# A graph network on one Trainium2 core: PE's stop at every seventh select removed, POOL's gathers tied to the selects that DVE has taken

## The chip, the cores and the metric

The kernel runs on one core of one Trainium2 chip. The metric is the device time of one execution in microseconds (us), as the median of several runs. The engines are called PE (TensorE), DVE (VectorE), ACT (ScalarE), POOL (GpSimd) and SP (SyncE, which only issues DMAs here).

## The reference

There are 6250 nodes with 128 features each and 200,000 edges, sorted by their destination. Edge messages are combined in two blocks, each with a layer norm before it and a residual after it:

```python
h = relu(layernorm(x))                       # block 1, src/dst as row/col
e = relu(h[row] @ W1[:128] + h[col] @ W1[128:] + b1)
mask = sigmoid(e @ W2 + b2)                  # one number per edge
w = mask / (segment_sum(mask, row)[row] + 1e-9)
agg = segment_sum(w * h[col], row)
x = x + relu(where(deg > 0, 0.5 * h + 0.5 * agg, h) @ Wl + bl)

h = relu(layernorm(x))                       # block 2, four layers
for layer in range(4):
    agg = segment_max(h[src], dst)           # 0 where a node has no edge
    h = relu(agg @ W + b + h @ R)
x = x + h
```

## The kernel before

Nodes stand in 49 tiles of 128, grouped into 7 ranges of 7 tiles (896 nodes). The work comes in stages: lists of neighbours are built first; then the edge stage computes `mask` for each edge (the block of the program with names `a_...`, lines 1055 to 1545); then a stage sums the weighted neighbours (`b_...`); then the four layers of the max block run (`c_...`, lines 1853 to 2370).

The edge stage and each of the four layers fetch neighbour rows in two ways at once.

**Selects.** One neighbour of a node in each of the 49 source tiles is fetched by a matrix product with a 0/1 matrix, the choice. For every range (7) and every source tile (49) there is one select, so 343 in the edge stage and 343 in a layer. A select (`select`, L1316 and L2151) is six matmuls on PE, three parts of the features by two column blocks of 512 and 384, into a PSUM buffer `wide`: there are two such buffers in the edge stage and three in the layers. DVE then takes the result (`take`, L1404 and L2242), one 128x896 instruction on `hidden` or on `even`/`odd`, and counts the semaphore `taken` up by one. PE waits for `taken` before it writes the same buffer again. The choice matrices of seven selects form a chunk. Three chunk buffers exist. In the layers SP loads them from DRAM (`load_choice`); in the edge stage DVE makes them (`compare`). After the last select of a chunk PE waits for its own matmuls and then counts `choice_used` up, which is what frees the chunk buffer:

```python
last.then_inc(selected, 1)
if s % CHUNK == CHUNK - 1:
    pe.wait_ge(selected, n + 1)
    pe.sem_inc(choice_used, 1)
```

**Gathers.** The neighbours that selects don't cover are fetched by POOL with indirect DMAs (`gather_tile`, L1199 and L2032). Each gathers 128 rows of 512 bytes into one slot of a ring, and there are 430 of them in the edge stage and in a layer, 2 to 25 for a tile (`CAP`). POOL takes the tiles in order. Before a tile it waits only until the tiles that lay in its ring slots have been reduced. The ring has 38 slots in the edge stage and 56 in the layers, so POOL may run ahead of DVE by that much.

**Order of the work.** Each engine's order is written out by the Python loops. DVE goes through the selects; where the count of gathers reached in proportion to the selects, plus a lag of 5 selects, ends tile u, it waits for the tile's gathers to land and reduces it (`reduced_at`, `weigh_tile`, `reduce`). In the edge stage POOL also scatters the tile's mask values to DRAM, one indirect DMA for each of the 430 columns (`store_tile`, L1211), five tiles behind the gathers. In the layers POOL stores the new features of a range with seven indirect DMAs (`store`, L2049) after the gathers of the fourth tile of the next range; those features are made at the earliest 16 selects after the range's reductions end (`STAGED_AT`, `STEP`; for the sixth range, the last with selects after it, that is select 323, where POOL has 22 gathers of the layer left). DVE's and PE's remaining steps of a range (joins, transposes, the two products) are placed at fixed selects.

Of the kernel before, what the change touches and what calls it, by code (L numbers as in the profile page):

```python
# [87 lines left out]
CAP_ALL = sum(CAP)  # L88
FIRST = tuple(sum(CAP[0:u]) for u in range(TILES))
# [33 lines left out]
def gnn(nc, x_in, src_in, dst_in, w1_in, b1_in, w2_in, b2_in, wl_in, bl_in,  # L123
# [20 lines left out]
    with ExitStack() as whole:  # L144
# [11 lines left out]
        sb, ps, sem = tensors(whole)  # L156
# [51 lines left out]
        with nc.cleanup_on_exit(), ExitStack() as ctx:  # L208
            sb, ps, _ = tensors(ctx)
            sem = nc.alloc_semaphore  # L210
# [813 lines left out]
        CHUNK = RANGE  # L1024
# [17 lines left out]
        def landed_counts(tiles, flows):  # L1042

            sums, counts = [0] * flows, []
            for n in range(tiles):
                sums[n % flows] += 16 * CAP[n % TILES]
                counts.append(sums[n % flows])
            return counts

        def reduced_at(u, lag):  # L1050

            n = -(-sum(CAP[0:u + 1]) * SELECTS // CAP_ALL) + lag
            return n if n < SELECTS - 1 else AT_END
# [4 lines left out]


        A_RING, A_FLOWS, A_LAG, A_BEHIND, A_PICKS = 38, 10, 5, 5, 6  # L1060
        A_PLACES, A_LANDED = ring_places(TILES, A_RING, A_FLOWS), landed_counts(TILES, A_FLOWS)
        WEIGHED_AT = tuple(reduced_at(u, A_LAG) for u in range(TILES))
        VALUED_AT = tuple(at + 3 if at + 3 < SELECTS else AT_END for at in WEIGHED_AT)
# [9 lines left out]
        with nc.cleanup_on_exit(), ExitStack() as ctx:  # L1073
# [39 lines left out]
            parts_made = sem("a_parts_made")  # L1113
            pick_loaded = [sem(f"a_pick_loaded{e}") for e in range(A_PICKS)]
            choice_made = sem("a_choice_made")
            choice_used = sem("a_choice_used")
            choice_stored = [sem(f"a_choice_stored{e}") for e in range(3)]
            selected = sem("a_selected")
            taken = sem("a_taken")
# [77 lines left out]
            @block.gpsimd  # L1197
            def _(pool):
                def gather_tile(u):  # L1199
                    at, after = A_PLACES[u]  # L1200
                    if after > 0:
                        pool.wait_ge(logit_made, after)
                    for j in range(CAP[u]):
                        pool.indirect_dma_start(ring[:, at + j, :], None, table_a,  # L1204
                                                bass.IndirectOffsetOnAxis(near[:, u, j:j + 1], 0)
                                                ).then_inc(landed[u % A_FLOWS], 16)

                def store_tile(u):
                    pool.wait_ge(value_made, u + 1)
                    for j in range(FIRST[u], FIRST[u] + CAP[u]):  # L1210
                        pool.indirect_dma_start(mask_cells, bass.IndirectOffsetOnAxis(cell[:, j:j + 1], 0),  # L1211
                                                value[:, j:j + 1], None).then_inc(cells_stored, 16)

                for u in range(TILES + A_BEHIND):
                    if u < TILES:
                        gather_tile(u)
                    if u >= A_BEHIND:
                        store_tile(u - A_BEHIND)
                bodies = bodies_of(pool)
                pool.sem_inc(far_used, 1)  # L1220
                with pool.Fori(0, bodies) as j:
                    pool.wait_ge(far_loaded, j * 32 + 32)
                    turn(pool, turns)
                    for s in range(GROUP):
                        pool.indirect_dma_start(far_rows[:, s, :], None, table_a,
                                                bass.IndirectOffsetOnAxis(far_slots[:, s:s + 1], 0)
                                                ).then_inc(far_gathered[s % 2], 16)
                    pool.wait_ge(far_valued, j + 1)
                    pool.wait_ge(cells_stored, CAP_ALL * 16)
                    turn(pool, turns)  # L1230
                    for s in range(GROUP):

                        pool.indirect_dma_start(mask_cells, bass.IndirectOffsetOnAxis(far_cell[:, s:s + 1], 0),
                                                far_value[:, s:s + 1], None, compute_op=ALU.add
                                                ).then_inc(far_added[s % 2], 16)
                        pool.wait_ge(far_added[s % 2], j * 32 + (16 + s // 2 * 16))
                        turn(pool, turns)
                    pool.sem_inc(far_used, 1)
# [68 lines left out]
            def _(pe):  # L1307
# [8 lines left out]
                def select(n):  # L1316
                    a, s, q, e = n // TILES, n % TILES, n % 2, n // CHUNK % 3
                    if a == 0 and s % CHUNK == 0:
                        pe.wait_ge(parts_made, 3 * (s // CHUNK + 1))
                    pe.wait_ge(choice_made, n + 1)  # L1320
                    if n >= 2:
                        pe.wait_ge(taken, n - 1)
                    for part in range(3):
                        for lo_c, hi_c in ((0, BANK), (BANK, RCOLS)):
                            last = pe.matmul(wide[q][:, lo_c:hi_c], parts[:, s, part, :],  # L1325
                                             choice[e][:, s % CHUNK, lo_c:hi_c], start=(part == 0),
                                             stop=(part == 2))
                    last.then_inc(selected, 1)
                    if s % CHUNK == CHUNK - 1:
                        pe.wait_ge(selected, n + 1)  # L1330
                        pe.sem_inc(choice_used, 1)

                def dot_own(a):
                    pe.wait_ge(bt_made, 2 * a + 2)
# [51 lines left out]
            def _(dve):  # L1386
# [8 lines left out]
                def compare(n):  # L1395
                    m, s = n // CHUNK, n % CHUNK
                    dve.wait_ge(pick_loaded[n % A_PICKS], (n // A_PICKS + 1) * 16)
                    if s == 0 and m >= 3:
                        dve.wait_ge(choice_used, m - 2)
                        dve.wait_ge(choice_stored[m % 3], m // 3 * 16)  # L1400
                    dve.tensor_scalar(choice[m % 3][:, s, :], pick_row[n % A_PICKS][:, :], one_up[:, :], None,  # L1401
                                      ALU.is_equal, saturate=False).then_inc(choice_made, 1)
# [447 lines left out]

        LAYERS = 4
        RING = 56
        FLOWS = 10
        LAG = 5
        STEP = 4
# [36 lines left out]
        with ExitStack() as ctx:  # L1892
# [30 lines left out]
            far_used = sem("c_far_used")  # L1923
            far_did = sem("c_far_did")
            choice_loaded = [sem(f"c_choice_loaded{e}") for e in range(3)]
            choice_used = sem("c_choice_used")
            source_loaded = [sem(f"c_source_loaded{e}") for e in range(2)]
            rest_made = sem("c_rest_made")
            parts_made = sem("c_parts_made")
# [35 lines left out]
            def _(sp):  # L1965
# [6 lines left out]
                def load_choice(n):  # L1972
                    a, c, e = n // CHUNKS_OF % RANGES, n % CHUNKS_OF, n % 3
                    if n >= 3:
                        sp.wait_ge(choice_used, n - 2)
                    sp.dma_start(choice[e][:, :, :].bitcast(U8),
                                 chosen[a, :, c * CHUNK:(c + 1) * CHUNK, :]).then_inc(choice_loaded[e], 16)

# [49 lines left out]
            def _(pool):  # L2028
# [3 lines left out]
                def gather_tile(layer, u):  # L2032
                    n = layer * TILES + u
                    at, after = PLACES[n]
                    if after > 0:
                        pool.wait_ge(reduced, after)
                    for j in range(CAP[u]):
                        pool.indirect_dma_start(ring[:, at + j, :], None, table1[layer % 2],  # L2038
                                                bass.IndirectOffsetOnAxis(near[:, u, j:j + 1], 0)
                                                ).then_inc(landed[n % FLOWS], 16)  # L2040

# [97 lines left out]
            def _(pe):  # L2139
# [11 lines left out]
                def select(layer, n):  # L2151
                    a, s = n // TILES, n % TILES
                    no, m = layer * SELECTS + n, (layer * SELECTS + n) // CHUNK
                    q, e = no % 3, m % 3
                    if a == 0 and s % CHUNK == 0:
                        pe.wait_ge(parts_made, 3 * (layer * CHUNKS_OF + s // CHUNK + 1))
                    if s % CHUNK == 0:
                        pe.wait_ge(choice_loaded[e], (m // 3 + 1) * 16)

                    if no >= 3:  # L2160
                        pe.wait_ge(taken, no - 2)
                    for part in range(3):
                        for lo_c, hi_c in ((0, BANK), (BANK, RCOLS)):
                            last = pe.matmul(wide[q][:, lo_c:hi_c], parts[:, s, part, :],  # L2164
                                             choice[e][:, s % CHUNK, lo_c:hi_c], start=(part == 0),
                                             stop=(part == 2))
                    last.then_inc(selected, 1)
                    if s % CHUNK == CHUNK - 1:
                        pe.wait_ge(selected, no + 1)
                        pe.sem_inc(choice_used, 1)  # L2170

                def turn_staged(layer, a, h, first, count):
                    no = range_no(layer, a)
# [226 lines left out]
```

## Time and profile before

| | |
|---|---|
| median of 3 runs | 6895.0 us (6875.02 to 6910.07) |
| profiled execution, first to last instruction | 6939.9 us |
| mean granted TensorE clock | 0.792 |
| PE busy | 3939.7 us (57%), 16577 matmuls |
| DVE busy | 4021.9 us (58%) |
| POOL busy | 3259.7 us (47%) |
| ACT busy | 858.7 us (12%) |

Of the profiled execution the page gives the span from its first to its last instruction. A busy share is an average over all stages. Counts in brackets (x) are instructions. "remote" as what ended a wait means that the profile names no instruction whose end released it; "issue" means that the engine waited for nothing that the profile shows. Matmul ends are modelled, and POOL's own semaphore and branch instructions are not counted as busy.

### The profile page before, as it was taken

How to read it: one execution, taken by the hardware profiler on the slowest of the kernel's cores; microseconds unless marked ns; L12 is line 12 of the kernel's file. 1: busy time of each engine (PE TensorE's matmuls, PEld its weight loads, DVE VectorE, ACT ScalarE, POOL GpSimd, SP SyncE). 2: the span in 40 equal slices, each digit the busy share in tenths (PEclk: the TensorE clock that was granted, in tenths of full speed). 3: DMA queues.
4: the chain of work that ended last, by engine and by line, in shares of the span. 5: the costliest groups of instructions: out<-in, count | busy, mean ns of one | idle time of the engine just before them, and what ended most of it. 6: DMA issues, size and time to landing. Idle time of an engine off the chain costs nothing.

```text
span 6939.9 us, 51665 instructions
## 1 busy us (share of the span) xinstructions
PE 3939.7 (57%) x16577; PEld 1823.3 (26%) x16577; DVE 4021.9 (58%) x6785; ACT 858.7 (12%) x2421; POOL 3259.7 (47%) x3300
## 2 busy tenths in 40 slices
PE   7631255535544698995565554565655565555565
PEld 5411122112211244442222221222222222222232
DVE  7799266535654688885555454454555454454454
ACT  0000000000000567763000001000010000000000
POOL 0300456756766334334455445555446555444544
PEclk9999577767777899997787777777777777687787
DMA  6468444323432899996322223222233222322221
GB/s 252 170 251 327 126 117 120 108 75 106 120 96 77 168 182 200 194 185 137 89 87 87 78 78 90 77 85 78 80 85 86 80 84 78 86 82 79 80 87 59
DMA packets 367939, 820.12 MB, mean 118 GB/s; under 512 B 101885, under 2 KB 222547, under 8 KB 367491
## 3 DMA queue, kind: packets, MB, share of 16 engines
q0 software_dynamic: 145712, 329.41, 21.7%
q1 hardware_dynamic: 172564, 408.70, 17.1%
q10 hardware_dynamic: 49392, 78.70, 3.9%
q8 instruction: 133, 2.18, 0.1%
q14 instruction: 138, 1.13, 0.0%
HBM read 579.98 MB, written 236.57 MB: 118 GB/s over the span
## 4 chain that ended last, share of the span: by engine, by line
PE 20%; another core or an unknown queue 20%; issue 7%; DVE 5%; POOL 0%; DMA 0%; ACT 0%; DVEq 0%; POOLq 0%
PE c_wide L2164 18%; DVE c_even L2252 2%; DVE c_ring L2276 1%; DVE c_odd L2252 1%; PE c_product L2196 1%; PE c_product L2197 1%; DVE c_source L2239 0%; PE c_turned L2208 0%; PE c_turned L2185 0%; DVE c_best_t L2259 0%; POOL table L2049 0%; DVE c_even L2249 0%; DVE c_staged L2281 0%; DMA c_source<-table 0%
## 5 line engine op out<-in xcount | busy, mean ns | idle before, releaser
L2164 PE MATMUL c_wide<-c_choice,c_parts 128*128 128x512 fp8e4 (+1 forms) x8232 | 1909.8, 392 | 1617.2 <-remote 727.9
L2038 POOL DMA_INDIRECT c_ring<-table,near x1720 | 1657.7, 964 | 995.4 <-issue 521.4
L2164 PEld LDWEIGHTS c_wide<-c_choice,c_parts 128*128 128x128 bf16 x8232 | 835.3, 106 | 2666.0 <-issue 1565.2
L2252 DVE TENSOR_TENSOR c_even<-c_even,c_wide 128x896 f32<-128x896 f32 x672 | 728.3, 1084 | 834.9 <-remote 635.6
L2252 DVE TENSOR_TENSOR c_odd<-c_odd,c_wide 128x896 f32<-128x896 f32 x644 | 698.0, 1084 | 778.1 <-remote 568.3
L1325 PE MATMUL a_wide<-a_choice,a_parts 128*128 128x512 fp8e4 (+1 forms) x2058 | 512.9, 398 | 506.2 <-DVE a_hidden L1411 265.5
L1411 DVE TENSOR_TENSOR a_hidden<-a_wide,a_minus_bt 128x896 f32<-128x896 f32 x343 | 372.0, 1085 | 623.3 <-remote 492.0
L1204 POOL DMA_INDIRECT a_ring<-table_a,near x430 | 470.1, 1093 | 450.1 <-DVE a_value L1472 279.3
L1733 PE MATMUL b_agg<-b_mass,b_h_row 128*128 128x512 f32 (+1 forms) x1372 | 595.3, 571 | 140.7 <-DMA b_mass<-masks 140.1
L1694 ACT ACTIVATE b_mass<-b_onehot,mask_r 128x128 f32<-128x128 bf16 x2058 | 625.5, 387 | 265.0 <-DVE b_onehot L1756 264.9
L1672 POOL DMA_DIRECT2D b_mass<-masks x343 | 297.4, 867 | 548.0 <-ACT b_mass L1694 508.4
L1211 POOL DMA_INDIRECT masks<-a_value,a_cell x430 | 447.2, 1040 | 138.7 <-issue 130.4
L1325 PEld LDWEIGHTS a_wide<-a_choice,a_parts 128*128 128x128 bf16 x2058 | 201.8, 106 | 827.0 <-issue 686.3
L2103 ACT ACTIVATE c_h_t<-c_product,c_b 128x512 f32<-128x512 f32 (+1 forms) x56 | 35.5, 634 | 2848.4 <-PE c_product L2197 2518.2
L1733 PEld LDWEIGHTS b_agg<-b_mass,b_h_row 128*128 128x128 f32 x1372 | 260.1, 198 | 455.5 <-issue 251.4
L2049 POOL DMA_INDIRECT table<-c_new,row_info x147 | 144.2, 981 | 501.2 <-ACT c_new L2112 466.1
L1778 DVE TENSOR_TENSOR b_pile<-b_pile,b_mass 128x896 f32<-128x896 f32 x224 | 244.3, 1091 | 159.4 <-DMA b_mass<-masks 158.7
L1756 DVE TENSOR_TENSOR b_onehot<-pick_of,up_row 128x768 bf16<-128x768 bf16 x343 | 326.2, 951 | 0.1
L1347 PE MATMUL a_logits<-a_hidden,a_w_col 128*32 128x512 f32 (+1 forms) x1372 | 189.4, 649 | 114.6 <-DVE a_hidden L1411 64.3
L2276 DVE TENSOR_TENSOR c_ring<-c_ring 128x256 f32<-128x256 f32 (+8 forms) x468 | 248.4, 531 | 0.3
L1401 DVE TENSOR_SCALAR a_choice<-a_pick_row,one_up 128x896 fp8e4<-128x896 bf16 x343 | 237.4, 693 | 0.0
L707 POOL DMA_INDIRECT meta<-record,rank x49 | 47.2, 963 | 381.8 <-DVE rank L777 367.4
(284 smaller groups left out, 3294.5 us busy)
## 6 DMA issues: line engine op xcount, KB each, us to landing
masks<-n_zeros SPq DMA_DIRECT2D x196, 784.0 KB, 20.5
b_mass<-masks POOLq DMA_DIRECT2D x343, 448.0 KB
c_choice<-chosen SPq DMA_DIRECT2D x196, 784.0 KB
a_pick_row<-picks ACTq DMA_DIRECT2D x343, 224.0 KB
chosen<-a_choice SPq DMA_DIRECT2D x49, 784.0 KB
c_ring<-table,near POOLq DMA_INDIRECT x1720
c_source<-table SPq DMA_DIRECT2D x28, 448.0 KB
a_ring<-table_a,near POOLq DMA_INDIRECT x430
```

The lines of the kernel that those rows point to most:

```text
L1204: pool.indirect_dma_start(ring[:, at + j, :], None, table_a, bass.IndirectOffsetOnAxis(near[:, u, j:j + 1], 0)).then_inc(landed[u % A_FLOW ...
L1211: pool.indirect_dma_start(mask_cells, bass.IndirectOffsetOnAxis(cell[:, j:j + 1], 0), value[:, j:j + 1], None).then_inc(cells_stored, 16)
L1325: last = pe.matmul(wide[q][:, lo_c:hi_c], parts[:, s, part, :], choice[e][:, s % CHUNK, lo_c:hi_c], start=(part == 0), stop=(part == 2))
L1411: dve.tensor_tensor(hidden[n % A_HIDDEN][:, :], wide[n % 2][:, 0:RCOLS], minus_bt[:, a * RCOLS:(a + 1) * RCOLS], ALU.max).then_inc(taken, 1)
L1672: pool.dma_start(flat[e], masks[u * P:(u + 1) * P, cb * RCOLS:(cb + 1) * RCOLS], accum_op=ALU.add).then_inc(mass_loaded[e], 16)
L1694: last = act.mul(mass[k % M_RING][:, c, :], onehot[e][:, c, :], mask_r[:, u, cb * RANGE + c:cb * RANGE + c + 1])
L1733: last = pe.matmul(agg[cb % 2][:, lo_c:hi_c], h_row[:, u, :], flat[e][:, lo_c:hi_c], start=(u == 0), stop=(u == TILES - 1))
L1756: dve.tensor_tensor(onehot[e][:, :, :], bc(pick_of[:, u, first:first + SCALED].unsqueeze(2), full), bc(up_row[:, :].unsqueeze(1), full), A ...
L2038: pool.indirect_dma_start(ring[:, at + j, :], None, table1[layer % 2], bass.IndirectOffsetOnAxis(near[:, u, j:j + 1], 0)).then_inc(landed[ ...
L2164: last = pe.matmul(wide[q][:, lo_c:hi_c], parts[:, s, part, :], choice[e][:, s % CHUNK, lo_c:hi_c], start=(part == 0), stop=(part == 2))
L2252: dve.tensor_tensor(side[:, :], side[:, :], found, ALU.max).then_inc(taken, 1)
L2276: halves.did(dve.tensor_tensor(lower, lower, upper, ALU.max))
```

## The change

PE's wait and its count of `choice_used` are taken out in both stages, and the semaphore with them. Who freed a chunk by it (DVE in the edge stage, SP in the layers) now waits for the count of finished selects, `selected`, itself. And POOL, ahead of every second gather from the 39th in the edge stage and from the 17th in a layer, waits until DVE has taken `g * 343 // 430 - ahead` selects, with `ahead` 0 in the edge stage and 2 in the layers.

```diff
+        def allowed_at(g, ahead):
+            return g * SELECTS // CAP_ALL - ahead
...
         A_RING, A_FLOWS, A_LAG, A_BEHIND, A_PICKS = 38, 10, 5, 5, 6
+        A_AHEAD = 0
...
-            choice_used = sem("a_choice_used")
...
                     for j in range(CAP[u]):
+                        g = FIRST[u] + j
+                        if g >= A_RING and g % 2 == 0:
+                            pool.wait_ge(taken, allowed_at(g, A_AHEAD))
                         pool.indirect_dma_start(ring[:, at + j, :], None, table_a,
...
                     last.then_inc(selected, 1)
-                    if s % CHUNK == CHUNK - 1:
-                        pe.wait_ge(selected, n + 1)
-                        pe.sem_inc(choice_used, 1)
...
                     if s == 0 and m >= 3:
-                        dve.wait_ge(choice_used, m - 2)
+                        dve.wait_ge(selected, CHUNK * (m - 2))
                         dve.wait_ge(choice_stored[m % 3], m // 3 * 16)
...
         RING = 56
+        AHEAD_BY, FREE = 2, 16
...
-            choice_used = sem("c_choice_used")
...
                     if n >= 3:
-                        sp.wait_ge(choice_used, n - 2)
+                        sp.wait_ge(selected, CHUNK * (n - 2))
...
                     for j in range(CAP[u]):
+                        g = FIRST[u] + j
+                        if g >= FREE and g % 2 == 0:
+                            pool.wait_ge(taken, layer * SELECTS + allowed_at(g, AHEAD_BY))
                         pool.indirect_dma_start(ring[:, at + j, :], None, table1[layer % 2],
...
                     last.then_inc(selected, 1)
-                    if s % CHUNK == CHUNK - 1:
-                        pe.wait_ge(selected, no + 1)
-                        pe.sem_inc(choice_used, 1)
```

## Rows read from the trace of the kernel before

**Rows 1.** Span and mean granted clock of the core.

```profile
core 0: 6939.9 us, clock 0.792
```

**Rows 2.** Windows: edge stage first, then the four layers, first select to last.

```profile
core 0: us, PE busy (x) PEld busy (x) DVE busy (x) ACT busy (x) POOL busy (x), PEclk, DMA share, GB/s
...
821.00:2230.00 1409.00, 718.52 (x3522) 261.70 (x3524) 783.42 (x1144) 43.38 (x82) 876.73 (x821) 0.74 0.35 104
...
3269.00:4154.00 885.00, 501.55 (x2234) 231.44 (x2232) 449.68 (x547) 36.16 (x55) 443.28 (x461) 0.76 0.29 83
...
4186.00:5069.00 883.00, 501.90 (x2186) 227.72 (x2184) 448.78 (x546) 28.79 (x41) 452.48 (x469) 0.75 0.28 81
...
5101.00:5972.00 871.00, 500.98 (x2186) 228.14 (x2184) 450.20 (x547) 28.79 (x41) 453.18 (x469) 0.77 0.29 83
...
6006.00:6908.00 902.00, 499.32 (x2185) 226.11 (x2183) 456.88 (x559) 23.07 (x29) 449.87 (x469) 0.76 0.28 80
```

**Rows 3.** The page: costliest groups of instructions.

```profile
L2164 PE MATMUL c_wide<-c_choice,c_parts 128*128 128x512 fp8e4 (+1 forms) x8232 | 1909.8, 392 | 1617.2 <-remote 727.9
L2038 POOL DMA_INDIRECT c_ring<-table,near x1720 | 1657.7, 964 | 995.4 <-issue 521.4
...
L2252 DVE TENSOR_TENSOR c_even<-c_even,c_wide 128x896 f32<-128x896 f32 x672 | 728.3, 1084 | 834.9 <-remote 635.6
...
L1204 POOL DMA_INDIRECT a_ring<-table_a,near x430 | 470.1, 1093 | 450.1 <-DVE a_value L1472 279.3
...
L1211 POOL DMA_INDIRECT masks<-a_value,a_cell x430 | 447.2, 1040 | 138.7 <-issue 130.4
...
L2049 POOL DMA_INDIRECT table<-c_new,row_info x147 | 144.2, 981 | 501.2 <-ACT c_new L2112 466.1
```

**Rows 4.** Windows of 5 us in one unbroken run of gathers (columns as in rows 2).

```profile
4788.00:4793.00 5.00, 4.70 (x27) 2.49 (x26) 4.13 (x6) 0.29 (x2) 3.76 (x4) 1.00 0.49 144
...
4798.00:4803.00 5.00, 0.40 (x3) 0.00 (x0) 1.78 (x4) 0.00 (x0) 3.78 (x5) 1.00 0.21 52
...
4818.00:4823.00 5.00, 0.00 (x0) 0.00 (x0) 0.00 (x0) 0.00 (x0) 3.78 (x5) 0.50 0.22 53
...
4838.00:4843.00 5.00, 3.44 (x10) 1.31 (x11) 3.53 (x4) 0.00 (x0) 0.00 (x0) 0.50 0.01 2
```

**Rows 5.** Waits, whole span: who waited for what, us in total, times, longest.

```profile
POOL c_ring L2038 <- issue: 521.4, 1680, 7.6
...
POOL c_ring L2038 <- DVE c_staged L2281: 469.4, 37, 31.2
```

**Rows 6.** Windows at two pauses of POOL and after them (columns as in rows 2).

```profile
5357.00:5360.00 3.00, 0.62 (x2) 0.28 (x3) 1.76 (x3) 0.00 (x0) 0.20 (x1) 0.50 0.00 0
5360.00:5365.00 5.00, 5.00 (x18) 2.14 (x17) 3.71 (x5) 0.00 (x0) 3.78 (x5) 0.65 0.16 43
...
5375.00:5380.00 5.00, 4.70 (x26) 2.37 (x25) 5.00 (x8) 0.00 (x0) 3.78 (x4) 1.00 0.67 213
...
3952.00:3955.40 3.40, 0.00 (x0) 0.00 (x0) 1.29 (x2) 0.00 (x0) 0.31 (x1) 0.50 0.09 22
...
3960.40:3965.40 5.00, 5.00 (x19) 2.17 (x18) 1.32 (x3) 0.00 (x0) 3.78 (x4) 0.64 0.53 194
```

**Rows 7.** Edge stage windows: all engines, then the takes of L1411 alone (DVE).

```profile
1259.00:1334.00 75.00, 53.84 (x294) 20.37 (x295) 68.25 (x81) 1.51 (x5) 59.66 (x50) 0.92 0.54 163
1334.00:1432.00 98.00, 18.95 (x71) 5.31 (x69) 10.30 (x14) 0.00 (x0) 74.51 (x77) 0.57 0.17 48
...
1259.00:1334.00 75.00, 33.62 (x32) 0.92 0.54 163
1334.00:1432.00 98.00, 6.48 (x6) 0.57 0.17 48
```

**Rows 8.** Line L2164: idle of PE ended by PE itself, us, times.

```profile
  PE c_wide L2164: 35.8, 89
```

**Rows 9.** Window: the last 49 selects of the third layer (columns as in rows 2).

```profile
5877.90:5971.90 94.00, 70.23 (x316) 32.53 (x314) 63.40 (x82) 2.22 (x4) 35.94 (x38) 0.85 0.28 87
```

## The prediction, on record before the changed kernel ran

> **What bounds the kernel now.** I read the stages first, then the costliest groups, then windows of 5 us inside the layers. The four layers take 885, 883, 871 and 902 us from first to last select, together 3541 of the 6939.9 us, and the edge stage takes 1409 us [rows 1, 2]. The change touches nothing else. In a layer no engine is near full: in 885 us PE is busy for 502, DVE for 450 and POOL for 443. A layer has 343 selects, so a select takes 885 / 343 = 2.58 us. Alone it needs far less: in the window from 4788 us PE runs 27 matmuls in 5 us, and at six to a select that is 1.1 us [rows 4]. DVE's take is 1.08 us [rows 3], and all that DVE does in a layer comes to 450 / 343 = 1.31 us a select.
>
> Where do the other 1.3 us go? The page's groups say that PE and DVE stand idle until "remote" [rows 3], which names nobody. Windows show it. In the run of gathers that starts at 4788 us, POOL issues four or five in each 5 us throughout. PE runs 27 matmuls in the first window, 3 in the one that starts 10 us later, none in the one that starts 30 us later. POOL stops before 4838 us, and from there PE and DVE move again [rows 4]. Nothing that the program states ties them together there: PE has its choice, and DVE waits for PE. So **a long unbroken run of POOL's indirect DMAs holds PE up**, little in its first 5 to 10 us and almost wholly after 20 us. I don't know by what path. Pauses cure it. After a pause that ends at 5360 us (3 us of it in the window before, 5 us in all) PE runs 18 matmuls in the next 5 us and 26 in those 15 to 20 us later, although POOL works all the while. After one of 3 us, which ends at 3955 us, it has 19 matmuls in the window 5 to 10 us later, at a mean clock of 0.64 [rows 6].
>
> The Trainium skill speaks against this reading: "SBUF — State Buffer", section "SBUF: two separate sides", has it that DMAs and engines use separate ports and that PE never waits for another engine at SBUF. By that rule gathers don't slow PE at SBUF and spreading them out gives nothing; the second rival below carries that case. The windows of rows 4 don't agree with a PE that nothing holds up, but they don't show the path either.
>
> **The pace of the gathers, layers.** Removed: runs as long as the 56 slots allow, 37 waits of 469 us in all for slots [rows 5]. Added: a wait at every second gather, so POOL stops within two gathers when DVE's takes stop. Its cost on POOL I take as nothing: the gathers that wait for a slot already carry such a wait. One issue is 0.96 us with 521 / 1680 = 0.31 us before it, 1.27 us [rows 3, 5]. POOL's work stays 430 gathers and 49 stores, 479 x 1.27 = 610 us a layer, or 1.40 x 1.27 = 1.78 us a select. If POOL is at work for a share d of the time, a select takes 1.78 / d. Now d = 610 / 885 = 0.69. So the question is how large d may be before PE is held up. Upper end: d = 1, 1.78 us, 610 us a layer. Lower end: d stays 0.69, no gain. Between them: 5 us of pause bought at least 20 us of work, d = 0.80, and 3 us bought at least 10, 0.77 [rows 6]. Both pauses had first to undo a long run that had brought PE to a standstill. With the gate no run gets that long, so I take 0.85: 1.78 / 0.85 = 2.09 us, 343 x 2.09 = 717 us a layer. Against 885 that is 168 less, in four layers 3541 - 4 x 717 = 673.
>
> Two checks on the 2.09 us. DVE's 1.31 us is below it. PE's clock was 0.76 in the layers [rows 2]; all at half clock a select would be 2.2 us, 755 us a layer, and that lies in my range. And in the last 49 selects of the third layer, where POOL issues only 38 DMAs in 94 us, a select takes 94 / 49 = 1.92 us at a clock of 0.85 [rows 9].
>
> **What the gate makes late.** A tile's last gather is let go 7 to 8 selects before DVE reduces the tile (lag 5, ahead 2), 15 us at 2.09. The seven stores of a range, 7 x 1.27 = 9 us, come between, so 6 us stay for the landing. POOL's wait for those stores (466 us in all [rows 3]) mostly goes, since it now comes to them after the features are made. After the last such stores (select 323) POOL has 7 + 22 = 29 DMAs, 37 us, and 20 selects are 42 us; then the landing and three small reductions. I add 5 us a layer, 20 in all; ends: 0 and 15 us a layer. At a layer's start 16 gathers go freely instead of 56, under cover of the lag.
>
> **The edge stage.** Here a select carries 860 / 343 = 2.5 indirect DMAs, the scatters included, and they aren't paced, only the gathers. From 1259 to 1334 us, 32 takes go beside 50 DMAs, 2.34 us each; in the next 98 us there are 77 DMAs and 6 takes [rows 7]. So the same thing happens, but POOL is nearer to being the bound. If all 343 selects ran at 2.34 us (803 us, with 535 DMAs beside them) and the other 325 DMAs ran alone at 1.27 (413 us), the stage would take 1216 us, 193 less. The other end is 0. The scatters keep runs of a tile's 9 or so DMAs, and DVE must wait for POOL anyway, so I take 60, nearer to nothing.
>
> **PE's stops.** The wait itself shows as 35.8 us of idle in 89 places of the layers, 0.4 us each [rows 8]; with 196 stops in the layers and 49 in the edge stage, 245 x 0.4 = 98 us is the upper end. But a select at 2.09 us is set by POOL, and PE has 1 us of slack in each, so I take 0. If that cover goes (d near 1 and PE at half clock), up to 98 us are gained. Who waits on `selected` instead, SP and edge-stage DVE, is let go at the same moment or a little earlier: 0. No DMA is added or moved on SP.
>
> **Sum.** 6939.9 - 673 + 20 - 60 = 6227 us for the profiled execution's span. The median of the runs is 6895, 45 less; so 6182, I say 6180.
>
> **Rivals.**
> 1. *The gate cures it wholly.* PE isn't held up at all in runs of two, and POOL sets the time: layers at 610 + 15 us, edge stage at 1216. That is 6895 - (3541 - 2500) - 193 = 5660. For it: the first 5 us of a run cost PE little. Against it: at d near 1 the gate never closes, and then runs are unbroken again. Chance 0.12.
> 2. *PE and POOL simply take turns*, or the hold-up comes from something else, so that d stays near 0.69 however the gathers are spaced. The time stays 6895, within 35 of it. Against it: the pauses of rows 6, after which both run. Chance 0.07; another 0.12 for little of it (d = 0.71 to 0.74, 6500 to 6860).
> 3. *Slower: the stock in the ring is missed.* The gate holds POOL back whenever takes stop, and what POOL doesn't do while PE stands it must do later, when DVE will wait for it at the reductions. A layer now has 610 us of POOL's work and 450 of DVE's in 885 us, so 610 + 450 - 885 = 175 us of it lie beside each other [rows 2]. If PE stays held up even by pairs and less than that overlaps, the layer gets longer; this is the point from which it decides. With half of the overlap lost it is 88 us a layer, 6895 + 352 = 7247; with all of it 7595. For it: the edge stage can't stop its scatters, and the wait for POOL is only 15 us away. Against it: DVE and PE work beside POOL for 20 us after a pause [rows 6]. Chance 0.07.
>
> The forecast, d from 0.75 to 0.95, has 0.62: 0.75 is 814 us a layer, and with nothing from the edge stage 6895 - (3541 - 3256) = 6610; 0.95 is 643 us a layer, and with 193 from the edge stage 6895 - (3541 - 2572) - 193 = 5733. The range holds this and a part of the case of little gain: 5750 to 6700. A measurement of this kernel can tell about 0.5% from no change, 35 us. Faster by more: 0.62 + 0.12 + 0.12 = 0.86; within: 0.07; slower: 0.07.
>
> **What would show it.** POOL's runs break into short ones: no 5 us window in mid-layer without matmuls; its waits at L2038 are no longer for reduced tiles but for takes, some 100 us a layer; its busy share in a layer rises from 0.50 to 0.6. The "remote" idle of PE and DVE falls to less than half. PE's idle ended by itself is gone. A layer takes about 720 us from first to last select, the gap to the next stays about 32 us, and the edge stage takes 1350. I'm wrong if a layer still takes over 830 us, if PE still stands for 10 us in runs that the gate has broken up, or if DVE's idle before reductions (lines 2276 and 2281) grows by more than 10 us a layer.

## The result, and the profile after

The changed kernel takes **6162.3 us** (median of 4 runs, 6151.6 to 6183.7). The kernel before took 6885.2 us in 4 runs, so the ratio is 0.8945 (95% interval 0.8906 to 0.8985): faster by 10.6%. The prediction was 6180 us, in a range of 5750 to 6700. The profiled execution took 6168.4 us, with a span of 6166.6.

The windows of the changed kernel come first: edge stage, the stage between it and the layers, then first to last select of each layer. They answer to [rows 2].

```profile
core 0: us, PE busy (x) PEld busy (x) DVE busy (x) ACT busy (x) POOL busy (x), PEclk, DMA share, GB/s
...
822.00:2135.00 1313.00, 715.37 (x3520) 259.87 (x3523) 784.15 (x1144) 43.38 (x82) 853.62 (x784) 0.76 0.38 111
2135.00:3189.00 1054.00, 825.21 (x2071) 398.18 (x2063) 766.53 (x1122) 636.44 (x2078) 421.13 (x456) 0.88 0.86 169
3213.00:3923.00 710.00, 511.01 (x2235) 234.76 (x2233) 449.58 (x547) 36.53 (x55) 454.00 (x461) 0.83 0.36 104
...
3954.00:4656.00 702.00, 501.25 (x2187) 227.79 (x2185) 450.06 (x547) 28.98 (x41) 460.75 (x469) 0.83 0.36 103
4689.00:5395.00 706.00, 507.00 (x2186) 226.92 (x2184) 449.19 (x547) 29.21 (x41) 460.44 (x469) 0.83 0.35 102
5427.00:6135.00 708.00, 506.69 (x2185) 226.50 (x2183) 456.23 (x559) 23.16 (x29) 460.25 (x469) 0.83 0.36 102
```

Each engine does the same work as before, in 702 to 710 us in place of 871 to 902. From the start of the first take to the start of the last, the four layers add up to 2822 us, 716 less than the 3538 of before. The mean clock of a layer went from 0.76 to 0.83, but PE's busy time hardly changed (501 to 511 us, before 499 to 502): what went is standing time. The groups of the page, which answer to [rows 3]:

```profile
L2171 PE MATMUL c_wide<-c_choice,c_parts 128*128 128x512 fp8e4 (+1 forms) x8232 | 1921.8, 392 | 872.7 <-issue 343.8
L2045 POOL DMA_INDIRECT c_ring<-table,near x1720 | 1689.8, 982 | 942.0 <-issue 493.7
...
L2256 DVE TENSOR_TENSOR c_even<-c_even,c_wide 128x896 f32<-128x896 f32 x672 | 727.5, 1083 | 486.5 <-remote 263.0
```

PE's idle before its selects fell from 1617 to 873 us, and DVE's before half of its takes from 835 to 487, of which "remote" from 636 to 263. POOL's busy time in gathers stayed, and even its idle time before them (995 to 942 us). What is different about its idle time shows in its waits in the layers, whose columns are total, times and longest:

```profile
engine line waited for: us in total, times, longest us
POOL c_ring L2045 <- issue: 481.8, 1450, 2.7
POOL c_ring L2045 <- DVE c_odd L2256: 226.6, 129, 13.6
POOL c_ring L2045 <- DVE c_even L2256: 207.3, 117, 6.2
POOL table L2056 <- ACT c_new L2119: 46.9, 5, 16.2
...
POOL c_ring L2045 <- DVE c_odd L2253: 6.6, 4, 4.8
```

Before, POOL paused 37 times at the gathers for 469 us [rows 5], and 466 us at its stores [rows 3]. Now it pauses 250 times at the gathers for 440 us, 1.8 us each, and 5 times at the stores for 47 us. **At the gathers the time is as long as before; it is cut finer.** What went is POOL's waiting at its stores (466 to 47 us) and at its DMAs of the output and of the far rows (279 to 5 us). POOL's work is the same in both kernels, so its waits in all must fall as a layer does.

Counting from the start of each matmul in the trace after the first select of the layers: before, there were 57 stretches of over 10 us in which PE started none, 960 us in all, and 154 of 728 windows of 5 us had none. After, there are 4 such stretches, 59 us, all at or behind a layer's last selects, and 19 of 584 windows, 11 of them inside a layer and away from its last 15 us.

The hold-up isn't gone. A run of gathers in the second layer of the changed kernel, in windows of 5 us:

```profile
4230.00:4235.00 5.00, 3.80 (x21) 1.78 (x20) 2.17 (x2) 0.00 (x0) 3.77 (x4) 1.00 0.19 54
4235.00:4240.00 5.00, 1.95 (x10) 0.64 (x8) 2.18 (x2) 0.00 (x0) 3.90 (x4) 0.90 0.70 211
4240.00:4245.00 5.00, 2.42 (x6) 0.73 (x6) 1.82 (x2) 0.00 (x0) 3.78 (x5) 0.50 0.16 55
4245.00:4250.00 5.00, 2.26 (x6) 0.73 (x6) 1.42 (x2) 0.00 (x0) 3.78 (x5) 0.50 0.17 45
4250.00:4255.00 5.00, 0.16 (x1) 0.00 (x0) 0.03 (x1) 0.00 (x0) 1.44 (x2) 0.50 0.13 34
4255.00:4260.00 5.00, 3.88 (x12) 1.64 (x13) 4.55 (x6) 0.00 (x0) 1.88 (x2) 0.55 0.05 13
```

It looks like [rows 4] on a smaller scale. POOL issues 4 or 5 indirect DMAs in each of the first four windows, PE goes from 21 matmuls to 6 and then 1, and they move again once POOL has stopped (its last issue before the pause starts at 4250.8). The clock fell to 0.50, that is 1.2 GHz, only after PE had slowed down.

One thing in these traces says more exactly what is late. Here are PE's selects and then DVE's takes one by one, in the kernel before and in the run of [rows 4]. The columns are start, length, instruction, how many, and in brackets the idle time before it and what ended it:

```profile
4804.33 4.90 PE L2164 MATMUL c_wide<-c_choice,c_parts 128*128 128x512 fp8e4 x18 [5.93 <-remote]
4811.56 1.31 PE L2164 MATMUL c_wide<-c_choice,c_parts 128*128 128x512 fp8e4 x6 [2.33 <-issue]
4824.86 2.42 PE L2164 MATMUL c_wide<-c_choice,c_parts 128*128 128x512 fp8e4 x6 [11.99 <-issue]
...
4810.41 1.09 DVE L2252 TENSOR_TENSOR c_even<-c_even,c_wide 128x896 f32<-128x896 f32 x1 [5.06 <-PE c_wide L2164]
4823.72 1.09 DVE L2252 TENSOR_TENSOR c_odd<-c_odd,c_wide 128x896 f32<-128x896 f32 x1 [12.21 <-remote]
4838.42 1.09 DVE L2252 TENSOR_TENSOR c_even<-c_even,c_wide 128x896 f32<-128x896 f32 x1 [13.61 <-remote]
```

The last matmul of the select that is taken at 4838.42 starts at 4808.9, and the count `selected` rises for it at 4838.4, 29 us later. PE starts its next select within 0.1 us of the end of each of these takes, so it stands because all three `wide` buffers are full. What the gathers delay is **the report that a select has finished**, and not the start of a matmul. Counted from the traces over all four layers: the six matmuls of a select never start more than 0.43 us apart, in the hold-up as without it. But before, 222 takes start over 2 us after their last matmul has started and DVE is free, 1470 us in all; in the changed kernel it is 179 takes and 698 us. Of the 117 takes of before that wait over 5 us, `selected` is seen to rise within 0.3 us of the take in 107. Whether the products themselves or only their report are late, the traces don't show, since matmul ends are modelled.

### The profile page after: what moved, and what is told of

It reads as the page before. It is cut to its first block and busy times, and to the rows that moved or that the text cites. A ratio compares the mean times of both kernels' runs of the same rounds, so it can differ in the third digit from the quotient of the medians.

```text
span 6166.6 us, 51521 instructions
## 1 busy us (share of the span) xinstructions
PE 3959.4 (64%) x16577; PEld 1827.8 (30%) x16577; DVE 4019.6 (65%) x6785; ACT 859.7 (14%) x2421; POOL 3308.5 (54%) x3300
## 5 line engine op out<-in xcount | busy, mean ns | idle before, releaser
L2045 POOL DMA_INDIRECT c_ring<-table,near x1720 | 1689.8, 982 | 942.0 <-issue 493.7
L457 POOL DMA_INDIRECT n_fetched<-nbrs,record x49 | 58.7, 1198 | 259.3 <-DVEq L524 244.7
```

## The experiments

Ten kernels were run, two of them twice, in four series. Each series has runs of the kernel before on its own chip, and these differ so much from series to series that only ratios within a series are compared. Where a kernel was executed only once, its stage times stand for it.

### First series: the parts alone, on a chip that held nothing up

**Stops alone:** the kernel before with PE's stops out, in both stages.

```diff
-                        pe.wait_ge(selected, no + 1)
-                        pe.sem_inc(choice_used, 1)
...
-                        sp.wait_ge(choice_used, n - 2)
+                        sp.wait_ge(selected, CHUNK * (n - 2))
```

> Only PE's stops are taken out, in both stages; the gathers run ahead as before. Theory (long unbroken runs of indirect DMAs hold PE up, and the gate breaks them): the runs stay as long, so 6885 us within 35, a layer 885 from first to last select. Rival (PE's wait for its own matmuls drains its queue, and that is what the gathers' time falls into): most of the 720 us is gained here, 6165 to 6400 us.

**Pace alone:** the changed kernel with the stops put back (the reverse of that edit).

> Only the gate on the gathers, in both stages; PE's stops stand as before. Theory: 6162 us plus what 245 stops cost where nothing hides them; POOL sets the pace of a select, so 0 to 30 us, 6160 to 6195 us. Rival (the stops matter): 6300 us or more. Upper end if no stop were hidden: 6162 + 98 = 6260 us.

**Layers alone:** the changed kernel without the gate of the edge stage.

```diff
-                        if g >= A_RING and g % 2 == 0:
-                            pool.wait_ge(taken, allowed_at(g, A_AHEAD))
```

> The gate in the layers alone; the edge stage's gathers run ahead as the ring allows, the stops are out in both. Theory: the edge stage goes back to what it was, POOL's last scatter 50 us later, so 6162 + 50 = 6212 us (6195 to 6235). Rival (the edge stage gained all of its 95 us between first and last select): 6255 us.

**No gathers:** the kernel before without the layers' 1720 gathers and DVE's waits for them. The ring is set to zero once and reduced as before, so the output lacks the neighbours that the gathers bring.

```diff
-                        pool.indirect_dma_start(ring[:, at + j, :], None, table1[layer % 2],
...
-                        dve.wait_ge(landed[n % FLOWS], LANDED[n])
+                        dve.wait_ge(ring_clear, 1)
```

> The kernel before with the gathers of the four layers left out; the output then lacks those neighbours. POOL still has the 49 stores of a layer. Theory: nothing holds PE up, a select takes what DVE's work and PE's product steps take, 1.31 us and a little for PE's half clock, so 343 x 1.31 to 1.45 = 450 to 500 us a layer, about 5250 us in all. Rival (the idle of PE and DVE has another cause than the gathers): layers stay above 800 us, over 6500 us.

| | median us | ratio (95%) | layers, first to last take |
|---|---|---|---|
| kernel before, 15 runs | 5553.2 (5543.7 to 5563.8) | | |
| stops alone | 5557.7 | 1.0009 (0.9999 to 1.0019) | 574, 584, 580, 584 |
| pace alone | 5593.6 | 1.0071 (1.0054 to 1.0087) | 583, 586, 586, 584 |
| layers alone | 5575.1 | 1.0035 (1.0022 to 1.0047) | 586, 587, 585, 587 |
| no gathers, one execution | 5031.1 | | 463, 461, 460, 461 |

I had not reckoned with the first row: the kernel before takes 5553 us here, 19% less than 6885. The page of the kernel with the stops out shows what sets the time (the chain of waits, then groups):

```profile
POOL c_ring L2033 28%; POOL table L2044 2%; POOL out_x L2048 1%; DMA c_source<-table 0%; PE c_wide L2159 0%; POOL c_far_rows L2059 0%; DVE c_even L2244 0%; DMA c_ring<-table,near 0%; DVE c_ring L2268 0%; DVE c_source L2231 0%; DVE c_odd L22
...
L2033 POOL DMA_INDIRECT c_ring<-table,near x1720 | 1694.9, 985 | 535.2 <-issue 529.7
...
L2244 DVE TENSOR_TENSOR c_even<-c_even,c_wide 128x896 f32<-128x896 f32 x672 | 725.0, 1079 | 45.8 <-PE c_wide L2159 41.5
...
L2268 DVE TENSOR_TENSOR c_ring<-c_ring 128x256 f32<-128x256 f32 (+8 forms) x468 | 249.4, 533 | 497.2 <-DMA c_ring<-table,near 496.7
```

Here POOL never waits for anyone: its idle is all issue, 0.31 us a gather. DVE waits 497 us for gathers to land and 46 us, not 835, before its even takes. A layer with the gap behind it (46 us) takes 620 to 630 us, close to the 610 us of POOL's work that the prediction worked out. And PE is not held up: no take starts over 0.6 us after its last matmul has started and DVE is free. Windows of this kernel in the third layer, where POOL issues without a pause (its longest unbroken run in the layers has 480 indirect DMAs and lasts 621 us):

```profile
4700.00:4705.00 5.00, 4.49 (x24) 1.96 (x23) 3.94 (x6) 0.00 (x0) 3.78 (x4) 1.00 0.51 141
4705.00:4710.00 5.00, 3.98 (x20) 1.73 (x21) 5.00 (x7) 0.00 (x0) 4.07 (x4) 1.00 0.31 111
4710.00:4715.00 5.00, 3.06 (x18) 1.40 (x15) 3.27 (x5) 0.00 (x0) 3.78 (x5) 1.00 0.53 138
4715.00:4720.00 5.00, 5.00 (x27) 2.38 (x26) 4.40 (x6) 0.00 (x0) 3.78 (x5) 1.00 0.33 127
```

(PE's count dips only where DVE takes late; the next stop, 10.5 us of DVE from 4719 us, is a wait for a landing.) So the hold-up is a condition that a chip is in or not. Without it the gate has nothing to win and costs 0.4% in the layers and 0.7% in all; a likely reason is that it stops the engine that sets the time. The expectations of this series assumed the hold-up, and what they say of a part's gain fell with it. With no gathers at all a layer takes 461 us, within the 450 to 500 expected and hardly more than DVE's 450: that is the floor. As the hold-up was absent here, this run doesn't test what causes it.

### Second series: what holds PE up, and what cures it

The kernel before took 6978.9 us here (7 runs), so the hold-up was there.

**Own pauses:** the kernel before; POOL waits after each 8th gather until that gather has landed, and for nothing else that is new.

```diff
+                        if (FIRST[u] + j) % 8 == 7:
+                            pool.wait_ge(landed[n % FLOWS], LANDED[n] - 16 * (CAP[u] - 1 - j))
```

> The kernel before, no gate on the takes and the stops in place, but in the layers POOL waits after every eighth gather until that gather has landed, a pause of some 2 us that has nothing to do with the selects. POOL may still run 56 slots ahead. Theory (what counts is how long a run is unbroken): runs of 8 and a pause are 12 us for 8 gathers, so PE is held up far less; a layer takes 700 to 780 us, 6885 - 4 x 145 = 6300 us (6180 to 6500). Rival (it is the tie to DVE's takes, or the lead, that helps): 6885 us or, with 53 pauses a layer of 2 us lost to POOL, up to 7000.

**Plain DMAs:** the kernel before; each of the layers' gathers becomes a plain DMA from POOL of 128 rows that lie together, the same number of bytes into the same slot. The output lacks the right neighbours.

```diff
-                        pool.indirect_dma_start(ring[:, at + j, :], None, table1[layer % 2],
+                        pool.dma_start(ring[:, at + j, :], table1[layer % 2][u * P:(u + 1) * P, :]
```

> The kernel before, with each gather of the layers replaced by a plain DMA from POOL of the same 128 rows of 512 bytes, one after the other in the table; the output is then the maximum over other rows. Theory A (any DMA that POOL issues in a long run does it): a layer stays at 885 us if the issue takes 1.27 us as before; if it is shorter, say 1.15, the layer has the same hold-up over less POOL time, 820 to 885. Theory B (the gather's indices are what matters): PE isn't held up, a layer takes 500 to 620 us.

**A longer lead:** the changed kernel, POOL allowed 20 selects ahead and 40 gathers free.

```diff
-        AHEAD_BY, FREE = 2, 16
+        AHEAD_BY, FREE = 20, 40
```

> The changed kernel with POOL let 20 selects ahead of the takes instead of 2, and 40 gathers free at a layer's start instead of 16. Theory (length of runs): after the free start the gate lets pairs go as takes come, as before, so runs are as short except at the start: 0 to 25 us more a layer, 6165 to 6260 us. Rival (what helps is that POOL keeps close to DVE, so that no stock builds up): the time goes most of the way back, over 6500 us.

**A wait at every 16th gather:** the changed kernel.

```diff
-                        if g >= FREE and g % 2 == 0:
+                        if g >= FREE and g % 16 == 0:
```

> The changed kernel with the layers' gate at every sixteenth gather instead of every second, same lead. Theory: runs are 16 gathers (20 us) or more, so the later part of each holds PE up; between 885 and 705 a layer, 740 to 820 us, 6300 to 6620 us in all. Rival (only the mean lead counts): within 35 us of 6162.

Own pauses: **6307.0 us, ratio 0.9031 (0.8998 to 0.9065)**, layers of 714, 722, 710 and 692 us. The expectation, 700 to 780 us a layer and 6180 to 6500 in all, held. This is the kernel before, with its ring and all its waits for slots, and nothing keeps POOL in step with the selects. Only the runs are broken. Its gathers' waits:

```profile
L2038 POOL DMA_INDIRECT c_ring<-table,near x1720: 938/944/2472, 3309.0 to 6288.0; - x192
...
  issue: 484.9, 1523
  DMA c_ring<-table,near: 435.7, 193
```

193 pauses of 2.3 us are enough for nearly the whole gain in the layers. Being in step with the takes is not what counts. But each pause ends with a landing, so this kernel also bounds how many gathers are on their way at once, and that was not tried apart.

Plain DMAs: 5320.2 us in one execution, layers of 464 to 467 us (500 to 620 expected where the indices are what matters), next to the 461 without any gathers. The hold-up was there in this run: its edge stage, whose DMAs are still indirect, took 1455 us, and most of what DVE waited for there is "remote" again:

```profile
L1411 DVE TENSOR_TENSOR a_hidden<-a_wide,a_minus_bt 128x896 f32<-128x896 f32 x343 | 372.2, 1085 | 668.8 <-remote 532.9
```

In windows of the last layer POOL issues twice as many DMAs as before, in a run of 65 that lasts 40 us:

```profile
5136.00:5141.00 5.00, 4.70 (x27) 2.54 (x26) 4.63 (x7) 0.00 (x0) 3.92 (x4) 1.00 0.65 201
...
5146.00:5151.00 5.00, 5.00 (x29) 2.60 (x27) 5.00 (x7) 0.00 (x0) 5.00 (x10) 1.00 0.87 277
...
5161.00:5166.00 5.00, 4.70 (x26) 2.21 (x25) 5.00 (x8) 0.00 (x0) 5.00 (x11) 1.00 0.73 216
...
5171.00:5176.00 5.00, 4.91 (x26) 2.52 (x27) 5.00 (x8) 0.00 (x0) 5.00 (x11) 1.00 0.82 270
```

PE keeps 26 to 29 matmuls in each at 201 to 277 GB/s, and DVE is never idle in the last three. In no take of the layers is the report of the select over 1.8 us late. With gathers PE had no matmul at 53 GB/s [rows 4]. The number of bytes, the writes into SBUF and a busy POOL are therefore not the cause; it is something in how the gathers fetch. Two things changed at once, the form of the instruction and rows that lie together in place of scattered ones, and which of the two counts was not tried apart.

The longer lead and the wait at every 16th gather gave 6507.3 and 6520.8 us in one execution each, layers of 779 to 791 and 784 to 800 us. Expected for the lead was almost the change's own time: that **fell**, and the number is the rival's (over 6500 us, because POOL no longer keeps close to DVE). The own pauses, which don't keep it close either, speak against the rival's reason. I had thought the wait at every second gather would stop POOL whenever takes stop. With a lead of 20 selects it does so only after the lead is used up, some 25 gathers later. The lead is itself a bound on how long a run goes on. The expectation for 16 held. POOL's pauses at the gathers of the layers side by side, with the longest run and the share of the indirect DMAs that lie in runs of 16 or more, counted from the traces from the first take of the layers to the last; a run ends where POOL stands over 0.5 us between two of them (the first and the last row are from the profiles of before and after, of another series):

| | pauses | us in all | longest run | share in runs of 16 or more | mean layer us |
|---|---|---|---|---|---|
| before | 37 | 469 | 56 DMAs, 73 us | 94% | 885 |
| wait at every 16th | 86 | 719 | 39, 51 us | 96% | 791 |
| lead of 20 selects | 159 | 423 | 46, 60 us | 69% | 788 |
| own pauses | 193 | 436 | 15, 19 us | 0% | 710 |
| the change | 250 | 440 | 34, 47 us | 49% | 706 |

The more pauses, the shorter the layer. Their total at the gathers doesn't order the rows: 423 us and 469 us give 788 and 885. The own pauses reach 710 us although DVE then waits for POOL's landings (337 us before the reductions), so the two good kernels end at the same time for different reasons: one lacks takes, the other lacks POOL's time. In the own pauses only 99 takes, 302 us in all, come over 2 us behind their matmuls.

### Third series: the parts again, with the hold-up there

The two parts alone, the same edits as in the first series.

> The kernel of e1 once more, since there the kernel before took 5553 us and its PE wasn't held up. On a chip where the kernel before takes about 6900 us, theory (the gate is the whole gain): within 0.7% of the kernel before. Rival (the stops carry part of it): 2% or more faster. On a chip like that of e1: within 0.2%, as there.

> The kernel of e2 once more. Where the kernel before takes about 6900 us, theory: a ratio of 0.895 to 0.905. Rival (the stops carry part of it): 0.92 or more. On a chip like that of e2: 1.007, as there.

| | median us | ratio (95%) | layers, first to last take |
|---|---|---|---|
| kernel before, 7 runs | 6910.1 (6880.3 to 6920.4) | | |
| stops alone | 6798.6 | 0.9845 (0.9813 to 0.9876) | 876, 838, 856, 870 |
| pace alone | 6181.9 | 0.8966 (0.8932 to 0.9001) | 714, 703, 708, 716 |

This was the **same chip as in the first series**, where this kernel had taken 5553 us. So the condition comes and goes on one chip; it isn't a property of the chip alone. The gate by itself is nearly the whole gain, and its ratio is in the 0.895 to 0.905 expected. The stops by themselves gain 1.6%, between the two cases expected (within 0.7%, or 2% and more). Beside the gate they are worth the difference of 0.8966 and 0.8945, 0.2%, and those intervals overlap; the two ratios are also from different series. The gate was not tried in the layers alone while PE was held up. In the profiles of this series the edge stage takes 1406 us from first to last take in the kernel with the stops out and 1299 in the one with the gate. The page of the kernel with the stops out (compare [rows 3]):

```profile
L2159 PE MATMUL c_wide<-c_choice,c_parts 128*128 128x512 fp8e4 (+1 forms) x8232 | 1949.4, 396 | 1485.5 <-issue 727.7
...
L2244 DVE TENSOR_TENSOR c_even<-c_even,c_wide 128x896 f32<-128x896 f32 x672 | 726.9, 1082 | 801.7 <-remote 584.8
```

PE's idle is 132 us less than in the profile of before (1617.2 to 1485.5), though the stops themselves showed only 35.8 us. The two profiles are of different series, so the difference is a hint. The traces show what it comes from. A stop waits for `selected`, the very report that the hold-up delays. The layers have 192 selects behind a stop, a layer's first left out. There PE starts 692 us in all after its buffer is free and its last matmul has started in the kernel before, against 42 us with the stops out. With the gate it is 433 us with the stops (this series) and 44 without (the change). Yet little of this reaches the time, because DVE's takes wait for the same late reports: over 2 us in 222 takes for 1470 us with the stops, and in 216 for 1434 us without.

### Fourth series: how long must a pause be?

An iota of 768 numbers on POOL after each 8th gather is a break in the stream of DMAs in which POOL stays busy. First in the changed kernel, then in the kernel before.

```diff
+                        if (FIRST[u] + j) % 8 == 7:
+                            fill.wait()
+                            fill.did(pool.iota(idle_i[:, :], [[1, 768]], base=0, channel_multiplier=0))
```

> The changed kernel, and in the layers POOL writes 768 counting numbers to a tile of its own (iota, estimated at 0.9 us from the 0.95 us of 800 numbers on one partition) after every eighth gather, so that no more than eight gathers and a store group go without a pause in the issue of DMAs. Theory (a short pause in POOL's indirect DMAs is enough, whatever POOL does in it): the runs that still exceed 10 us in the changed kernel are cut, POOL's work is 608 + 54 x 1.2 = 673 us a layer, 680 to 705 us a layer, ratio to the kernel before 0.885 to 0.895. Rival (POOL must be idle, or idle for some 2 us): the hold-up stays and POOL's work is longer, 720 to 770 us a layer, ratio 0.90 to 0.93.

> The kernel before, no gate, stops in place, with the same iota after every eighth gather in the layers. Theory (a short pause in the issue is enough): as in e5, whose pauses of 1.8 us gave 710 us a layer, with less POOL time: 690 to 740 us a layer, ratio 0.89 to 0.92. Rival (POOL must be idle for some 2 us): hold-up as in the kernel before with 65 us more of POOL's work, a ratio of 0.99 to 1.03.

One tile's instructions, from the kernel before with the iota:

```profile
L2047 POOL IOTA c_idle_i<- x212: 782/787/800, 3287.3 to 6805.8; 128x768 int32 x106
```

The kernel before on this chip took 6997.6 us. With 212 breaks of 0.79 us: 6869.3 us, ratio 0.9828 (0.9785 to 0.9870), layers of 853 to 863 us. As many breaks as in the kernel with its own pauses, and about a sixth of its gain: between the theory's ratio (0.89 to 0.92) and the rival's (0.99 to 1.03), and near the rival's. From one DMA's end to the next one's start it is 0.96 us at such a break, 0.31 us elsewhere, and 1.9 us (median) at the own pauses. So counting pauses isn't enough: 0.79 us of other work hardly undoes the hold-up, about 2 us of idling did. Whether length, idling or the landing that ends an own pause counts was not separated. The changed kernel with the iota took 6186.0 us, ratio 0.8853 (0.8821 to 0.8886). That is the lowest ratio measured, but its layers take 704 to 706 us, as the change's 700 to 709 do, and its kernel before was slower by 1.6% than the change's. I don't call it better. The number is the theory's too (0.885 to 0.895), but with the gate in place it doesn't tell the theory from the rival; the kernel without the gate does. No version was shown to beat the change.

## Why the prediction was right, step by step

- **The hold-up.** "A long unbroken run of POOL's indirect DMAs holds PE up" stood where the hold-up was there: broken runs alone gave 0.9031, and plain DMAs in their place layers of 465 us. That a run is broken isn't enough by itself: breaks of 0.79 us gave only 0.9828. It has two limits that I didn't see: it needs the indirect gathers (their form or their scattered rows), and it needs a condition of the chip that was absent in the first series. That the condition was there when the change was timed is luck: in the first series the gate alone had a ratio of 1.0071. And what is held up is the report of finished selects, up to 29 us in the run of [rows 4]; PE stands because its buffers are full. The Trainium skill's rule that I weighed against it ("SBUF — State Buffer", section "SBUF: two separate sides": PE never waits for another engine at SBUF) isn't contradicted at SBUF, since writes of the same bytes by plain DMAs cost PE next to nothing (layers of 465 us, 461 without gathers). It just doesn't cover what happens here.
- **POOL's share d = 0.85, 2.09 us a select.** Measured 479 x 1.27 / 706 = 0.86, and 706 / 343 = 2.06 us. The step that was chosen between far ends came out right: -716 us where the sum had -673 + 20. The rows bounded d only by 0.77 and 0.80 from below and 1 from above, so that it came within 0.01 is partly luck.
- **Lateness, +20 us.** Nothing was late: DVE shows no idle before its reductions (0.3 us at line 2280, none at 2285), and the gap between layers stayed at 32 to 34 us. A term of 0, its lower end.
- **The edge stage, -60.** First to last take became 95 us shorter (1408 to 1313), but the next stage starts by POOL's last scatter, and that came only 50 us earlier (2254.4 to 2204.2). The scatters (line 1218) that are left over after the last take, which the sum didn't name:

```profile
core 0: us, POOL busy (x), PEclk, DMA share, GB/s
2135.00:2210.00 75.00, 51.40 (x53) 0.55 0.05 5
```

  Before, 19 were left. The first select of the layers came 56 us earlier. The total was right by luck: a gain larger than 60 was partly given back.
- **The stops, 0.** Within the change, 0.2% at most, as said. Alone it was wrong: 1.6% or 112 us (86 to 129 by the interval), about the upper end of 98. The step that failed is the cover: I took PE's slack of 1 us a select from a kernel that POOL paces. In the kernel before PE is what is late. And the 35.8 us that the price came from are far too few: PE comes 692 us late behind the stops of the layers, most of it idle that the profile doesn't put down to PE itself.
- **The sum.** 6939.9 - 716 - 56 = 6168 against a span of 6166.6. The predicted 6227 is 60 us more: 43 from the layers' 673, 20 from the lateness, less 4 from the edge stage, and 1 of rounding.
- **The rivals.** "Cured wholly" (5660) did not come: the longest runs under the gate are still 34 DMAs, and PE still slows in them. But 5553 us in the first series is what it looks like with no hold-up at all, gate or not. "Turns" (6895) fell with the result, and with the 0.9031 of the own pauses. "Slower, stock missed" didn't show: DVE never waits for a landing. A slower side exists all the same, by another mechanism than I priced: 0.7% where nothing is held up.
- **The signs.** POOL's waits for takes: 440 us, 110 a layer (some 100 said). Its share of a layer: 0.64 to 0.66 (0.6). Remote idle of the even takes: 0.41 of before (under half). PE's own wait: gone. Missed: "no 5 us window without matmuls in mid-layer"; there are 11.

## What to carry to other kernels

When an engine stands idle for nobody that the program names, line up short windows of all engines and look at what the others do in an unbroken run. Compare when the work that it waits for started with when its count rose; then test it by breaking the run and by swapping the kind of work, as two experiments. Where the hold-up is there, background gathers by indirect DMA are worth a pause of some 2 us after every few (every 8th here), and a gate on the consumer's progress gives such pauses for nothing as long as its lead is short. Always time the kernel before beside the new one, on the same chip and at the same time: here the gate alone is worth 10.3% or costs 0.7%, on one chip, at two times.

## What the runs showed of the hardware that I had not expected

- On one chip, the kernel before took 5553 us in one series and 6910 us in a later one, each within 0.6% over its runs. At three other times, on at least two other chips, it took 6885, 6979 and 6998. What sets this condition is open.
- Indirect DMAs of scattered rows (0.94 us each plus 0.31 us of issue) and plain DMAs of rows that lie together (0.58 us each), the same number of bytes from the same engine, differ in what they do to PE: layers of 885 and 465 us.
- In the hold-up matmuls go on starting, and the count that the last one raises comes up to 29 us after its start (in the run of [rows 4]); with plain DMAs or without the condition of the chip no take starts over 1.8 us late.
- A 0.79 us break filled with an iota hardly helps (0.983), a pause of 2.3 us spent waiting does (0.903). The path by which the gathers reach PE stays open.
